# Sums of four heads through DRAM into 128 rows of 16, inverted there, and spread back by transfers, in a clipped attention

## The reference, cut to what matters

```python
scores = jnp.einsum('bhsd,bhtd->bhst', q, k) / scale
scores = jnp.clip(scores, -50.0, 50.0)
...
scores = jnp.where(attend, scores, -10000.0)
scores = jnp.clip(scores, -50.0, 50.0)
probs = jax.nn.softmax(scores, axis=-1)
...
ctx = jnp.einsum('bhst,bhtd->bhsd', probs, v)
ctx = ctx.transpose(0, 2, 1, 3).reshape(B, S, H)
```

## Time and profile before

| what | us |
|---|---|
| median of 3 runs | 3355.14 (3348.61 to 3356.6) |
| the profiled execution, its own time | 3352.55 |
| its span in the profile | 3350.5 |
| mean granted PE clock over the span | 0.896 of full |
| DVE busy, whole span | 2482.1 |
| PE busy, whole span | 2675.5 |
| the stage: first score to last low half | 2427.35 to 2657.89 |

### The profile page before, as it was taken

One profiled execution on the slowest core, in us unless ns is written; L12 is line 12 of the kernel. 1 busy time (PEld: TensorE's weight loads), 2 busy tenths in 40 slices (PEclk: granted clock), 3 DMA queues, 4 the chain that ended last, 5 costly groups with the idle time before them and its releaser, 6 DMA issues. The chain is left out here.

```text
span 3350.5 us, 62405 instructions
## 1 busy us (share of the span) xinstructions
PE 2675.5 (80%) x21148; PEld 1391.2 (42%) x21148; DVE 2482.1 (74%) x4757; ACT 1909.9 (57%) x2773; POOL 602.2 (18%) x539
## 2 busy tenths in 40 slices
PE   4868999686799999999996777776698756759983
PEld 3444444333365656565663433333311132224542
DVE  5756677666799999999995666634299798986548
ACT  2554433232499999999995433331387534845541
POOL 4440000012100010101013233312111260030013
PEclk7988999897899999999998888888799877869996
DMA  4433420200000000000000200010133010031301
GB/s 151 174 145 121 151 77 38 91 0 16 19 13 7 13 7 13 7 13 8 7 1 16 88 1 0 0 63 16 44 86 82 26 51 0 1 101 39 66 8 54
DMA packets 65338, 151.98 MB, mean 45 GB/s; under 512 B 11840, under 2 KB 20048, under 8 KB 63376
## 3 DMA queue, kind: packets, MB, share of 16 engines
q1 hardware_dynamic: 62368, 140.43, 14.1%
q0 software_dynamic: 2800, 9.18, 0.8%
HBM read 93.61 MB, written 24.38 MB: 35 GB/s over the span
## 5 line engine op out<-in xcount | busy, mean ns | idle before, releaser
L1617 DVE TENSOR_REDUCE s_top<-ps 128x1 f32<-128x512 f32 x1024 | 656.2, 682 | 30.3 <-PE ps L1512 30.0
L1586 ACT ACTIVATE s_prob<-ps,s_shift,m_sq 128x1024 int16<-128x1024 f32 x512 | 614.7, 1201 | 29.9 <-DVE s_shift L1625 29.9
L1512 PE MATMUL ps<-s_ks,s_qs 128*128 128x512 f16 x1024 | 352.5, 386 | 60.6 <-issue 14.1
L1517 PEld LDWEIGHTS ps<-ident,s_prob 128*128 128x128 f16 x4096 | 272.2, 98 | 123.1 <-DVE m_o L1635 52.3
L1517 PE MATMUL ps<-ident,s_prob 128*128 128x128 f16 x4096 | 313.8, 220 | 0.7 <-ACT s_prob L1586 0.5
L1505 PE MATMUL ps<-s_ks,s_qs 128*128 128x512 f16 x1024 | 306.5, 381 | 0.8 <-ACT s_prob L1586 0.5
L1592 ACT ACTIVATE s_probT<-ps 128x1024 f16<-128x1024 int16 x256 | 261.9, 1023 | 5.8 <-PE ps L1517 4.8
L1008 PE MATMUL ps<-m_hT,m_w 128*128 128x512 f16 x1024 | 231.8, 381 | 1.8 <-PEq L105 1.8
L249 PE MATMUL ps<-ident,s_parts 128*128 128x128 f16 x640 | 75.5, 290 | 130.0 <-POOL s_parts L240 128.1
L2289 DVE TENSOR_SCALAR s_prob<-ps,s_cap 128x1024 f32<-128x1024 f32 x128 | 158.2, 1269 | 25.4 <-PE ps L2198 25.3
L1630 DVE CAST s_probT<-ps 128x1024 f16<-128x1024 int16 x256 | 174.1, 680 | 3.4 <-PE ps L1517 3.4
(11 more groups left out here) (407 smaller groups left out, 5622.4 us busy)
## 6 DMA issues: line engine op xcount, KB each, us to landing
s_qs<-m_qT SPq DMA_DIRECT2D x144, 128.0 KB, 2.5
s_ks<-m_kT SPq DMA_DIRECT2D x96, 128.0 KB, 2.4
numbers<-s_numbers SPq DMA_DIRECT2D x21, 512.0 KB, 3.0
s_slabs<-numbers SPq DMA_DIRECT2D x21, 512.0 KB, 4.4
m_ks<-context_parts SPq DMA_DIRECT2D x12, 512.0 KB, 7.5
expert_rows<-s_y SPq DMA_DIRECT2D x19, 256.0 KB, 2.0
s_rows_in<-in_ctx SPq DMA_DIRECT2D x16, 256.0 KB, 3.0
x_sb<-in_L_ffn_W_up SPq DMA_DIRECT2D x4, 1024.0 KB, 7.2
```

Source lines behind the costliest of these rows:

```text
L1512: pe.matmul(quarter_at(q), qs[:, hb, bass.ds(t * P, P)], ks[:, hb, cols(q, 512)], start=True, stop=True).then_inc(s.top_scored, 1)
L1517: j = pe.transpose(turned(half, F16)[:, cols(m, P)], prob[:, u, cols(8 * half + m, P)].bitcast(F16), k.ident[:])
L1586: act.activation(prob[:, u, cols(half, HALF)], pair(half).rearrange("p m n -> p (m n)"), ACT.Exp, bias=shift[:, u:u + 1], scale=sq[:, bass ...
L1617: dve.tensor_reduce(top4[:, u, q:q + 1], quarter_at(q), AX.X, ALU.max).then_inc(s.top_read, 1)
```

## The change

Of the 16 quarters, 15 no longer have their inverse taken of all 128x512 numbers, of which 32 rows of each head are alike. For quarter i:

1. SP stores four rows of 512 sums (one for each head) to a scratch in DRAM, waits, loads them as 128 rows of 16 into `compact`, and waits (`gather_sums`).
2. DVE inverts the 128x16 numbers.
3. POOL stores them to DRAM (L2289 of the changed kernel), waits, spreads each head's 512 numbers over 32 rows of `inv` with four transfers (L2293), waits, and then multiplies as before (L2300).

The last quarter is inverted as before. `INVERT` goes from 5 to 8 and `ROUNDED` from 9 to 16. SP runs `gather_sums` behind the loads of pairs 2, 4 and 6, and for quarters 12 to 14 at its end.

```diff
-    A, R, LAG, LATE, INVERT, ROUNDED = 3, 5, 1, 3, 5, 9
+    A, R, LAG, LATE, INVERT, ROUNDED = 3, 5, 1, 3, 8, 16
+    LAST = H // 4 * B - 1
...
+        compact = s.sb("compact", [P, B, 4 * S // P], F32)
...
+            def gather_sums(i):
+                c, b = i // B, i % B
+                sp.wait_ge(s.sums_ready, (2 * c + 1) * B + b + 1)
+                sp.dma_start(k.inverse[b, :, :], sums[0:P:HD, b, :]).then_inc(s.sums_stored, 16)
+                sp.wait_ge(s.sums_stored, 16 * (i + 1))
+                sp.dma_start(compact[:, b, :], k.inverse[b, :, :].rearrange("a (j e) -> (a j) e", j=HD)
+                             ).then_inc(s.sums_loaded, 16)
+                sp.wait_ge(s.sums_loaded, 16 * (i + 1))
+
             for pair in range(PAIRS):
...
+                if pair >= 2 and pair % 2 == 0:
+                    for b in range(B):
+                        gather_sums((pair // 2 - 1) * B + b)
+            for i in range(LAST - B + 1, LAST):
+                gather_sums(i)
...
                 pool.wait_ge(s.inverted, i + 1)
+                if i:
+                    pool.wait_ge(s.divided, i)
+                if i < LAST:
+                    pool.dma_start(k.inverse[B + b, :, :].rearrange("a (j e) -> (a j) e", j=HD), compact[:, b, :]
+                                   ).then_inc(s.inverse_stored, 16)
+                    pool.wait_ge(s.inverse_stored, 16 * (i + 1))
+                    for a in range(4):
+                        pool.dma_start(inv[cols(a, HD), :], k.inverse[B + b, a, :].partition_broadcast(HD)
+                                       ).then_inc(s.inverse_spread, 16)
+                    pool.wait_ge(s.inverse_spread, 64 * (i + 1))
                 pool.wait_ge(s.num_ready, (2 * c + 1) * B + b + 1)
...
-                dve.wait_ge(s.sums_ready, (2 * c + 1) * B + b + 1)
-                if i:
+                if i < LAST:
+                    dve.wait_ge(s.sums_loaded, 16 * (i + 1))
+                    dve.reciprocal(compact[:, b, :], compact[:, b, :]).then_inc(s.inverted, 1)
+                else:
+                    dve.wait_ge(s.sums_ready, (2 * c + 1) * B + b + 1)
                     dve.wait_ge(s.divided, i)
-                dve.reciprocal(inv[:], sums[:, b, :]).then_inc(s.inverted, 1)
+                    dve.reciprocal(inv[:], sums[:, b, :]).then_inc(s.inverted, 1)
```

More of the change, by code:

```diff
@@ L2150, in attention_clipped @@
     STEPS = ITEMS * KT
-    A, R, LAG, LATE, INVERT, ROUNDED = 3, 5, 1, 3, 5, 9
+    A, R, LAG, LATE, INVERT, ROUNDED = 3, 5, 1, 3, 8, 16
+    LAST = H // 4 * B - 1
     with stage(k, "even_loaded", "odd_loaded", "mask_loaded", "cap_steps", "scored", "clipped", "exp_ready", "mixed",
-               "ones_ready", "sums_ready", "num_ready", "inverted", "divided", "hi_ready", "lo_ready") as s:
+               "ones_ready", "sums_ready", "num_ready", "sums_stored", "sums_loaded", "inverted", "inverse_stored", "inverse_spread", "divided", "hi_ready", "lo_ready") as s:
         loaded = (s.even_loaded, s.odd_loaded)
@@ L3045, in gated_layers @@
         k.expert_rows = nc.dram_tensor("expert_rows", (ROUTED * P, D), F32).ap()
+        k.inverse = nc.dram_tensor("inverse", (2 * B, 4, GT), F32).ap()
         k.numbers = nc.dram_tensor("numbers", (21 * P, SLAB), F16).ap()
```

## The result

| | before | after |
|---|---|---|
| median of the runs | 3353.45 (4 runs) | 3394.58 (4 runs, 3392.49 to 3395.82) |
| span of the profiled execution | 3350.5 | 3392.8 |
| ratio | | 1.0126, 95% interval 1.0114 to 1.0138 |

Slower by 1.26%, 41 us; the forecast was 3409, range 3374 to 3441. The span grew by 42.3 us. Where these 42.3 lie can be read off four marks of the timelines: clip 7, the last clip, the last low half, and the next stage's first load (L205).

A forecast was written before the change was run, and what follows sets the result against it. DVE was taken to set the pace where reciprocals stand, PE elsewhere. -23.5 + 48.8 + 23.2 + 6 = +54.5 us on the profiled 3352.55, plus 2.6 for the median, gave 3409.6, stated as 3409; range 3374 to 3441.

The forecast's parts named there:

- The gain: On DVE, smaller reciprocals let clips keep PE's pace, so the last clip comes earlier: -23.5 us.
- The chain: POOL's low half, transfers and product run serially with ACT's high half; stalls before the last clip: +48.8 us.
- S: Time of POOL's store and spread with their waits, from low half to next product: taken as 8.8 us.
- the forecast's own case: Main case for POOL's transfers: S between 6 and 11.6 us, chance 0.67.
- The clock: PE loses full clock in stalls, 2 us for each group of four quarters: +6 us, between 0 and 12.
- The tail: Behind the last clip, POOL's products of quarters 12 to 14 delay the last full reciprocal: +23.2 us.
- The sum in S: Whole change without the clock's cost is 12 x S - 57; each microsecond of POOL's transfers counts twelve times.
- SP's two transfers: SP's store and load of the sums take 4.0 to 5.0 us, in time for DVE's small reciprocal: cost 0.
- cheap transfers: Rival: POOL's small transfers land as fast as SP's quickest, S 4.2, sum -6 us, 3349; chance 0.09.
- DVE holds POOL up: Rival: POOL issues only between two clips, pitch 1.53 us, sum grows by 19 to 3428; chance 0.08.
- The gathers come late: Rival: SP's two transfers exceed 7 us and DVE waits; at 8 us some +10, 3419; chance 0.06.
- expensive transfers: Rival: each POOL transfer takes over 3.9 us to landing, time beyond 3440; chance 0.10.

The follow-up runs named there:

- lag2_last_full: Changed kernel with POOL's low half two quarters later, `out` a ring of three, high halves at 20 steps, last four quarters with full reciprocals: 3339.2 us, ratio 0.9959.
- low_later: Changed kernel with POOL's low half of each quarter moved behind the next quarter's product: 3355.05 us, ratio to before 1.001.
- no_stacks: Changed kernel without SP's loads of queries and keys for pairs 2 to 7, so its output is wrong: 3376.53 us (one run).

## Why the prediction was right

- **The gain, -23.5.** Right. A small reciprocal is 0.24 us, and where nothing stalls a clip starts every 1.53 us. lag2_last_full shows the whole of it: 188.04 us, the forecast pace (184.0) plus two full reciprocals at 1.8.
- **The chain, +48.8.** The mechanism is right in every part that was named: nine waits of ACT for POOL's product, 3.1 to 5.7 us each, 41.0 together; none for the first quarter of a group; low_later takes them from 41.0 to 11.4 with the transfers in place, and lag2_last_full to none. The term was mis-sized by its S, 8.8 against 7.1 measured. With 7.1, 3 x (3 x 4.23 - 1.5) = 33.6. The pitch of POOL's issues was taken as 1.0 and is 0.49; the landing was taken as 2.9 and is 1.8 and 2.3, up to 3.7 and 4.1 in a crowd. The rows of gathers were the wrong neighbours for an undisturbed direct transfer: those of SP were nearer. An undisturbed S is 5.7, under the S of 6 at which the forecast's own case begins. That SP's loads of the next pair fall on two of three chains in each of the first two groups was not foreseen, and it brought the average back up; no_stacks puts it at 15 us.
- **The clock, +6.** The stalls up to the last clip cost 16.65 + 23.5 = 40.2 us, 6.6 more than the 33.6 of the chain. That is the size of this term, but no run separates the clock from other small losses, and that it is the clock's doing is not shown.
- **The tail, +23.2.** It is 17.2. Quarters 12 to 14 need S of 6.9, 5.8 and 6.1 where three of 8.8 were taken, 7.6 us less. Some 1.6 of it are given back: ACT comes to quarter 12's high half, behind the last copies out of PSUM, 2.1 us after its product.
- **The sum in S.** 12 x 7.1 - 57 is +28.2; with the 6 us of the clock +34.2. The marks show 16.7 + 17.2 = 33.9.
- **SP's two transfers, 0.** Right but for 3.3 us behind the last clip, in parallel with POOL's chain. From a store of 8 KB to the load behind it pass 1.7 us, and a load lands in 1.5 to 1.7.
- **Not in the prediction: the drain, +6.2.** The end of the stage was taken as unchanged. This is the one whole term that was missed.
- **The rest.** The stage began 2.5 us later, with the same code ahead of it; over all runs clip 7 starts between 2433.1 and 2440.7, whichever the kernel, so this is a spread of executions and no effect. 2.5 + 16.7 + 17.2 + 6.2 = 42.6, and the span grew by 42.3.
- **What was luck.** S was put too high, which made chain and tail 21 us too dear, and the drain of 6.2 us was not in the sum. These two go against each other and leave the forecast 12 us above the measured 42.3. The crowding was not in the sum either: had the undisturbed S been priced rightly, at 5.7, the sum would have been 12 x 5.7 - 57 + 6 = +17, and the too high S covered for it.

The rivals: *cheap transfers* needed S under 4.76; undisturbed it is 5.7, and no_stacks is still 23 us slower than before. The Trainium skill's fixed cost of about 2.0 us for a transfer issued by GpSimd (page "DMA: Bandwidth & Descriptors", section on the anatomy of a SWDGE DMA) was nearer than my 2.9: the traces show 1.8 and 2.3. What made the estimate of S from it too short are three more issues of 0.49 us and the crowd. *DVE holds POOL up*: the pitch of 0.49 us, also where the four issues stand beside clips (2474.41 to 2476.42), excludes it. *The gathers come late* did not come (3.2 us for the two of them, not 7), nor did *expensive transfers*: only the last of four spreads in a crowd went past 3.9 us to landing.

## What to carry to other kernels

Before a slow operation is replaced by transfers, follow the order on the engine that issues them: if it waits there for the transfers and, in the same round, for an engine that waits for its result, each microsecond of latency is paid once per round, however idle the engine is. Once the dependent step stood two rounds later, the same transfers cost nothing here ahead of the last clip; what was left was the drain and a longer tail. And ask first whether the slow operation only stands too close together: two halves over twice the steps gave the same gain as the transfers in the best order tried, with none of them.

## What the runs showed of the hardware that was not expected

- POOL's drain at the end of a stage grows by 0.083 us for each transfer that POOL issued in it, long after they landed: 3.30 us for 40, 4.9 for 60, 6.2 for 75.
- A small direct transfer of POOL: issue 0.58 us for the store and 0.49 for a spread, landing 1.8 and 2.3 us (medians; without SP's loads 1.7 and 2.2). Beside SP's loads, with the DMA engines 92 to 98% busy, up to 3.7 and 4.1.
- One spread of 256 KB from four rows lands in 5.2 us, four of 64 KB in 2.3 each, and where it is used SP's loads take up to 8.3 us to land instead of 4.2.
- POOL's power of 128x512 takes 81.9 us, where DVE's reciprocal takes 3.35.
